# Flamingo block on one core: queries of two batches at once, P times V by head pairs, the mean of V from an added zero row

## The reference, cut to what matters

```python
# x (32, 224, 512), ctx (32, 750, 384), mask (32, 224): True where a query is kept
x = x + tanh(g_xattn) * attention(layernorm(x), ctx, mask)
x = x + tanh(g_ffn) * bit_ffn(layernorm(x))

# attention, 16 heads of 32
q = (x @ Wq.T), k, v = split(y @ Wkv.T)
attn = einsum('bhnd,bhmd->bhnm', q * scale, k)
attn = where(pad_mask[:, None, :, None], attn, -1e9)   # a row that isn't kept: all scores equal
out = einsum('bhnm,bhmd->bhnd', softmax(attn), v)      # ... so it gets the mean of V
```

## Time and profile before

| | |
|---|---|
| median of three runs | 2137.53 us |
| profiled execution | 2138.34 us, span of its trace 2136.5 us |
| PE busy | 1908.6 us (89%) |
| DVE, ACT, POOL busy | 1278.7 us, 1067.5 us, 557.7 us |
| first part | PE from 27.59 to 1593 us |
| second part | from 1597.09 us to the end |

### The profile page before, as it was taken

How to read it: one execution, slowest core, us unless ns; L and a number is a source line. 1 busy time by engine, 2 the same in 40 slices (tenths; PEclk the granted TensorE clock), 3 DMA queues, 4 the chain that set the end, 5 groups by cost and what they waited for, 6 DMA issues and landing times. The chain is left out here.

```text
span 2136.5 us, 47614 instructions
## 1 busy us (share of the span) xinstructions
PE 1908.6 (89%) x17554; PEld 1489.4 (70%) x17611; DVE 1278.7 (60%) x2524; ACT 1067.5 (50%) x1923; POOL 557.7 (26%) x621
## 2 busy tenths in 40 slices
PE   4999999989999997999899979999966888888887
PEld 4888888868888886778778867888753444444443
DVE  4445454434445544545454544555448999999996
ACT  3344444434434443334344433444326888888887
POOL 2101011010101111111111111112006777777774
PEclk9999999989999998999999989999978999999999
DMA  3021111131211113111111031111212222222221
GB/s 107 29 70 37 38 37 38 37 90 38 69 41 37 37 37 89 37 38 37 38 58 51 26 90 47 37 38 37 65 34 90 85 88 88 88 88 86 81 84 55
DMA packets 56158, 122.65 MB, mean 57 GB/s; under 512 B 5527, under 2 KB 5527, under 8 KB 55864
## 3 DMA queue, kind: packets, MB, share of 16 engines
q1 hardware_dynamic: 55992, 120.07, 17.5%
HBM read 101.63 MB, written 29.43 MB: 61 GB/s over the span
## 5 line engine op out<-in xcount | busy, mean ns | idle before, releaser
L565 DVE TENSOR_TENSOR k_l<-psum,k_h 128x376 fp32r<-128x376 f32 (+1 forms) x256 | 140.1, 547 | 339.6 <-ACT k_h L395 339.2
L560 DVE TENSOR_REDUCE nmax<-psum 112x1 f32<-112x750 f32 x256 | 228.4, 934 | 189.7 <-PE psum L757 189.7
L404 ACT ACTIVATE prob<-psum,nmax 112x750 f32<-112x750 f32 x256 | 224.8, 882 | 232.0 <-DVE nmax L560 232.0
L337 POOL TENSOR_SCALAR x_var<-x_mv 56x1 f32<-56x1 f32 x32 | 8.1, 253 | 1218.1 <-DVE x_mv L538 1218.1
L395 ACT ACTIVATE k_h<-psum 128x376 fp32r<-128x376 f32 (+1 forms) x256 | 123.8, 484 | 339.6 <-PE psum L768 339.6
L768 PE MATMUL psum<-y_h,wkv_h 128*128 128x376 f32 (+1 forms) x768 | 277.3, 361 | 0.0
L778 PE MATMUL psum<-wkv_h,y_h 128*125 128x512 f32 x576 | 250.8, 435 | 27.4 <-DVE q_l L553 27.4
L768 PE MATMUL psum<-y_l,wkv_h 128*128 128x376 f32 (+1 forms) x768 | 255.8, 333 | 0.0
L768 PE MATMUL psum<-y_h,wkv_l 128*128 128x376 f32 (+1 forms) x768 | 255.7, 333 | 0.0
L1280 PE MATMUL psum<-w_q,hq_t 128*128 128x512 bf16 x841 | 192.9, 382 | 62.0 <-DVE hq_t L1183 62.0
L778 PE MATMUL psum<-wkv_l,y_h 128*125 128x512 f32 x576 | 236.7, 411 | 0.0
(11 more groups left out here) (123 smaller groups left out, 3485.1 us busy)
## 6 DMA issues: line engine op xcount, KB each, us to landing
y<-in_ctx_t SPq DMA_DIRECT2D x32, 1125.0 KB, 6.2
w_part<-in_w_t SPq DMA_DIRECT2D x32, 512.0 KB, 4.9
xb<-in_x SPq DMA_DIRECT2D x56, 256.0 KB, 2.7
ab<-attn_rows SPq DMA_DIRECT2D x56, 256.0 KB, 2.9
out_rows<-yo SPq DMA_DIRECT2D x56, 256.0 KB, 2.1
attn_rows<-vmean_rows SPq DMA_DIRECT2D x32, 336.0 KB
xa<-in_x SPq DMA_DIRECT2D x32, 112.0 KB
attn_rows<-attn SPq DMA_DIRECT2D x32, 112.0 KB
```

The costliest lines, as they stand in the source:

```text
L404: act.activation(prob[:, e, :], ps_score[e][0:RP], ACT.Exp, bias=nmax[:, i:i + 1], accum_out=den[:, i:i + 1]).then_inc(p.exp, 1)
L560: dve.tensor_reduce(nmax[:, i:i + 1], ps_score[e][0:RP], AX.X, ALU.max, negate=True).then_inc(p.max, 1)
L565: dve.tensor_tensor(k_l[:, g, s0:s1], ps_proj[k_bank[g, hf]][:, 0:s1 - s0], k_h[:, g, s0:s1].bitcast(F32), ALU.subtract).then_inc(a_kl, 1)
```

## The change

- The 56 rows of `x` of two batches are loaded, normalised, transposed and multiplied by Wq together, once for a pair of batches. Each batch gets one more row between, which is zero: `RM = R + 1 = 57` rows, `RP = 114` for a pair. For DVE the normalisation falls in even periods, the query matmuls and the split of q in odd ones.
- A zero row of `x` gives equal scores, so row 57 of each batch's output is the mean of V. `y_sum`, the group's matmuls and `after_group` go. In each period SP stores the 56 rows and the mean row, waits until both have landed, and issues the DMA that spreads the mean over 168 rows.
- P times V works on pairs of heads: 12 matmuls a group instead of 24, with 64 columns of V as weights and 114 columns moving. Half of each result is not wanted (head 0 of V with head 1 of P); `heads_out` on DVE picks the diagonal with two instructions (L618, L620) where one copy stood.
- The first scores of a period wait for the first two K pieces only, `k0 - (2 * NG - 2)`; what follows waits for the others.
- The programs of even and odd periods are written apart. K piece (1, 1) comes ahead of the V pieces 3 and 4 on PE, `k_half(1, 1)` and `v_chunk(3)` ahead of `normalise` on DVE, and two of ACT's three `next_y` ahead of the third softmax pair.
- The nested loops become two single ones with a `middle` between them, in which the mean of the absolute weights is made.

```diff
-    RP = 2 * R
+    RM = R + 1
+    RP = 2 * RM
...
+                def results(b):
+                    sp.wait_ge(last.on, b + 1 + ONE)
+                    sp.dma_start(rows(attn_d, b, RB), attn[0:R, :]).then_inc(last.st, 16)
+                    sp.dma_start(vmean_d[bass.ds(b, 1), :], attn[R:RM, :]).then_inc(last.st, 16)
+                    sp.wait_ge(last.st, 32 * (b + 1) + ONE)
                     sp.sem_inc(met_sp, 1)
-                    with sp.Fori(0, QTR) as t:
-                        b = sp.snap(q * QTR + t)
-                        f = sp.value_load(kind[0:1, bass.ds(b, 1)])
-                        with sp.If(f > 1):
-                            sp.sem_inc(a_fill, 16)
-                        with sp.Else():
-                            sp.dma_start(rows(attn_d, b, 0, RB), vmean_d[bass.ds(b, 1), :].to_broadcast([RB * R, D])).then_inc(a_fill, 16)
-
-                sp.wait_ge(a_flag, 4)
-                batches(sp, period, fills)
+                    sp.dma_start(rows(attn_d, b, 0, RB), vmean_d[bass.ds(b, 1), :].to_broadcast([RB * R, D])).then_inc(a_fill, 16)
...
+                def heads(p, n):
+                    act.wait_ge(p.q, n + 1 + ONE)
+                    for s in range(2):
+                        for e in range(2):
+                            act.activation(q_h[:, s, :, e, :], ps_q[:, :, RM * s:RM * s + RM], ACT.Copy,
+                                           scale=head_col[:, e:e + 1]).then_inc(p.qh, 1)
...
-                    dve.tensor_copy(o_t[:, g, :], ps_o[:, g, :]).then_inc(p.oe, 1)
-
-                def divided(p, n):
+                    dve.tensor_scalar(o_t[:, g, :], ps_o[:, g, 0:RM], head_one[:, 0:1], 1.0, ALU.mult, ALU.mult).then_inc(own_o, 1)
+                    dve.wait_ge(own_o, 1)
+                    dve.scalar_tensor_tensor(out=o_t[:, g, :], in0=ps_o[:, g, RM:RP], scalar=head_one[:, 1:2], in1=o_t[:, g, :],
+                                             op0=ALU.mult, op1=ALU.add).then_inc(p.oe, 1)
+                    dve.sem_clear(own_o)
...
+                def even(b, t, late):
...
+                    heads_out(last, b, 1)
+                    if more_pairs(t, 1):
+                        moments(last, t + 1, 32 * (t + 2) + ONE)
+                    weights(b, late)
+                    k_half(m, 0, 1, 1)
+                    v_chunk(m, 0, 1, 3)
+                    if more_pairs(t, 1):
+                        normalise(last, t + 1, (t + 1) * (2 * NBLK) + RB)
+                    second_half(last, n1, 2, 0)
+                    second_half(last, n1, 2, 1)
+                    negated_max(last, n0, 3, 0)
+                    negated_max(last, n0, 3, 1)
+                    heads_out(last, b, 2)
...
                     for j in range(MJ):
-                        for h in range(HPG):
-                            w = 128 * g + HD * h
-                            mm = pe.matmul(ps_o[HD * h:HD * h + HD, g, :], v[:, slot, j, w:w + HD],
-                                           prob_t[:, g % 2, h // 2, j, R * (h % 2):R * (h % 2) + R],
+                        for e in range(2):
+                            w = 128 * g + PW * e
+                            mm = pe.matmul(ps_o[PW * e:PW * e + PW, g, :], v[:, slot, j, w:w + PW], prob_t[:, g % 2, e, j, :],
                                            start=(j == 0), stop=(j == MJ - 1))
...
-                def ordered(b, j, q, attends, projects):
-                    n0 = b * NP + ONE
-                    m = b + 1
-                    here, ahead = j, (j + 1) % 2
-                    pe.wait_ge(a_kl, 2 * NG * m + ONE)
-                    if attends:
+                def even(b):
+                    n0, m = b * NP + ONE, b + 1
+                    k0 = 2 * NG * m + ONE
+                    pe.wait_ge(last.ql, 2 * b + 4 + ONE)
+                    pe.wait_ge(a_kl, k0 - (2 * NG - 2))
+                    pe.wait_ge(last.pa, n0)
+                    pe.wait_ge(last.pd, n0)
+                    scores(last, 0, 0)
+                    pe.wait_ge(a_yl, CC * (b + 2) + ONE)
+                    pe.wait_ge(a_kl, k0 - 1)
+                    v_chunk(0, 1, 0)
+                    pe.wait_ge(a_kl, k0)
+                    k_half(0, 1, 0, 0)
...
+                    scores(last, 0, 2)
+                    weighted(last, n0, 0, 1)
+                    pe.wait_ge(a_va, MH * m + 2 + ONE)
+                    k_half(0, 1, 1, 1)
+                    pe.wait_ge(a_kl, k0 + 3)
+                    v_chunk(0, 1, 3)
+                    turn_prob(last, n0, 2, 0)
+                    turn_prob(last, n0, 2, 1)
+                    pe.wait_ge(a_kl, k0 + 4)
+                    v_chunk(0, 1, 4)
+                    turn_out(last, b, 1)
+                    pe.wait_ge(last.pa, n0 + 6)
+                    pe.wait_ge(last.pd, n0 + 6)
+                    scores(last, 0, 3)
```

More of the change, by code:

```diff
@@ L344, in _, with period @@
                 rstd(last, 0)
-                def period(b, j, q, t):
+                def period(b, j, t, late):
+                    if j == 0 and more_pairs(t, 1):
+                        rstd(last, t + 1)
                     if loads_ahead(b):
-                        rstd(last, b + 2)
                         split_y(b + 2, j)
-                batches(pool, period, lambda q: None)
+                batches(pool, period, lambda: None)
                 def slow(b, n):
@@ L459, in ordered @@
                     if projects:
-                        k_half(m, 2, 0)
-                        k_half(m, 2, 1)
+                        k_half(m, 1, 2, 0)
+                        heads(last, t + 1)
                     if attends:
@@ L498, in slow @@
                         turned(rest, i)
-                        heads(rest, i, 0)
+                        heads(rest, i)
                         for g in range(NG):
@@ L621, in ordered, with odd @@
+                def odd(b, t, late, attends, projects):
+                    n0, n1, m = b * NP + ONE, b * (2 * NP) + ONE, b + 1
                     if attends:
@@ L645, in ordered @@
                         heads_out(last, b, 1)
-                    if ahead:
-                        moments(last, b + 2)
-                    if has_part(b):
-                        weights(b, q, t, j)
-                    if ahead:
-                        normalise(last, b + 2, (b + 2) * NBLK + RB)
+                        weights(b, late)
                     if projects:
-                        heads(last, m, slot)
-                        k_half(m, 1, 1)
+                        k_half(m, 1, 1, 1)
+                        v_chunk(m, 1, 0, 3)
                     if attends:
@@ L692, in after_group, with period, middle @@
+                        k_half(m, 1, 3, 0)
+                    if attends:
+                        divided(last, b, 32 * b + ONE)
+                    if projects:
+                        k_half(m, 1, 3, 1)
+                def period(b, j, t, late):
+                    if j == 0:
+                        even(b, t, late)
+                    else:
+                        odd(b, t, late, has_part(b), projects_ahead(b))
+                def middle():
                     dve.tensor_reduce(w_sum[:], w_sums[:, 0:4 * DC].rearrange("p (i c) -> p i c", i=2), AX.X, ALU.add).then_inc(a_wsum, 1)
-                    dve.wait_ge(a_wmm, q + 1 + ONE)
+                    dve.wait_ge(a_wmm, 1 + ONE)
```

649 lines of the change are left out of this document (360 added, 289 removed).

## The result

The changed kernel took 2026.88 us (median, 2025.12 to 2028.69), the kernel before 2137.07 in the same comparison: a ratio of 0.948 (95% interval 0.947 to 0.950). I had said 2129, with a range from 2098 to 2162. The direction was right and the size was not: the forecast missed 102 of the 110 us. Three single executions far outside (3752.9 and 3259.8 us of the kernel before, 8838.0 us of one experiment) are in none of the ratios.

A forecast was written before the change was run, and what follows sets the result against it. It took PE's stream plus PE's gaps to bound the first part. Early pairs +13, late pairs +14, last pair -1, group ends -43, ends +8 gave -9 us, so 2129 us, range 2098 to 2162.

The forecast's parts named there:

- The gap before even periods: PE's first scores of even periods: 2.50 us idle at the loop's jump, and 1.5 us of slow clock, would remain.
- The new stall on DVE: PE in even periods would wait for DVE, held up by POOL's `y_l`: 1.9 us an early pair, 5.2 a late one.
- P times V: Head pairs with 114 columns take 1.33 us a group, +0.61 a group, +4.9 us a pair.
- the rival that the tiles don't overlap: The two 64-column tiles of P times V run one after the other: 2.5 us a group, total 2279; chance 0.04.
- Query: Query matmuls for two batches on PE: a pair pays 3.60 us once, -3.6 us a pair.
- First scores: The 1.15 us gap before odd periods goes, the jump before even ones remains: -1.15 us a pair, bounds 0 and -2.
- Group ends: Pairs ending a group of 8 batches lose their excess from SP's issues and the late y load: -43 us, bounds -38 and -47.
- Ends: Prologue +2, last batch +1.5, second part starting 4.5 us later: +8 us, bounds 3 and 12.
- Last pair: The last pair of periods, without POOL work: -1 us.
- DVE is never late: Rival: DVE and POOL miss each other, K (1, 1) is in time, every pair is PE-bound: 2079 to 2100; chance 0.13.
- the late wait for `k_l` before V 4: In late even periods PE waits 3.4 us before V 4 for DVE's quantised K (1, 1).
- the wait before scores 3: In even periods PE waits for DVE's `prob_t` copies before scores 3: 1.9 us early, 0.5 late.

The follow-up runs named there:

- 1809: Changed kernel, P times V as 24 matmuls of 32 weight columns: 2066.25 us with 114 moving columns, 1998.31 us with 57 and one copy per group.
- 1713: Changed kernel with P times V by single heads in three of four groups, head pairs in the fourth: 2017.95 us.
- 1665: Changed kernel with single heads in three groups of even periods and two of odd ones, `normalise` moved behind the copies: 1995.73 us.
- 1626: Kernel before with P times V over 4 of the 6 context pieces only: 2096.95 us.
- 1617: Changed kernel with P times V by single heads in two of four groups: 1992.66 us; with `normalise` moved behind the copies too, 1974.70 us.
- the shift by 128: Changed kernel, single heads in five of eight groups, `normalise` later, plus 64 small matmuls (128 instructions) ahead of TensorE's first loop: 1988.24 us against 1995.73.
- the pair of runs with equal code: Changed kernel with 24 matmuls of 32 weight columns: all 114 moving columns, 2066.25 us, against 57 moving and one copy per group, 1998.31 us.
- the best kernel here: Changed kernel with single heads in two of four groups and `normalise` moved behind the copies: 1974.70 us, 0.9231 of the kernel before.

## Why the prediction was wrong

*The gap before even periods: the step that failed.* I wrote "in even periods the jump remains" and took 2.50 us and 1.5 us of slow clock for a price of jumping. It is the price of fetching the loop's code again. The body went from 1882 to 1425 instructions, and the fetch went with it. The lengths in between (1809, 1713, 1665, 1626, 1617), the count of packets and the shift by 128 show it. In my sum it stayed in each pair with 4.0 us, taken over from the 92.5 and 95.4 of the kernel before: 15 x 4 = 60 of the 102 us. With the length alone put back the changed kernel lost 39 us, 3.6 in an early pair and 1.9 in a late one; the other 21 are gaps of about 2.0 us instead of 2.5 there and, by estimate 10 of them, the slow clock, which is absent behind most late gaps there and present in the kernel before. The row that could have told was on the page of the kernel before: 149 packets, 2.44 MB, for a first part with 13 jumps back. I never asked what they carried.

The Trainium skill bears on this, and I had not looked there. Its page "Runtime: NRT & Kernel Launch", section "Instruction fetch mechanics", says that TensorE's instruction memory takes 2048 instructions, that it is filled in blocks of 16 KiB, and that a taken branch whose target isn't in the window forces a fetch. The runs agree on the block (16 KB a packet) and on the branch (nine packets and 1.8 to 2.4 us in the changed kernel). They don't agree, for TensorE, with the same section's "only 2 cache lines" (which it works out from 32 KiB) and window of two pages, or with "Advanced Engine Details and Errata", section "ISA Cache", which says "Only 2 cache lines!" beside 128KB for TensorE: by two blocks each of these loops would be fetched again at every pass, and bodies of 1617 and 1425 instructions cost no packet. By 2048 instructions 1809 and 1713 should have stayed, and they did not, though with their 31 semaphore instructions they are only 1840 and 1744.

*The new stall on DVE: mis-sized.* I had 1.9 us a pair early and 5.2 late (with its clock); it was 0.35 and 1.68 and cost no clock: 8 x 1.55 + 7 x 3.5 = 37 us of the miss. The place was right (the scores of group 3, for DVE's copies of `prob_t`), and so was the cause: `xa` takes 1.98 us beside POOL's `y_l` instead of 0.55, and with `normalise` moved the wait is gone. That `y_l` is what makes `xa` long is read from the rows side by side (1.98 to 2.00 us beside it, 0.55 without); no run took `y_l` away. What was wrong is when POOL starts. Its `y_l` stand behind `x_var` and `x_rstd`, and these wait for DVE's moments and then take 0.71 and 1.50 us beside DVE's quantising; so the first `y_l` began at 977.73, when the third quantising step ran. None of the three waited (0.76, 0.70, 0.69 against my 0.7, 2.7, 2.1), V 4 waited for nothing, and `x_keep` took 0.19 early and 0.70 late, not 1.72. I had let three instructions meet POOL that the earlier trace rows show meeting it in another order of work.

*P times V.* 1.33 us a group, as taken; the rival that the tiles don't overlap fell. The columns cost 68 us in the pair of runs with equal code, 78 in my sum. The page on TensorE that I weighed there (the Trainium skill, "TensorE: Matmul & The Clock Gate", section LDWEIGHTS) gives 1.28 us for either form, so that this edit would cost nothing; the trace has 0.72 against 1.33 us.

*Query.* 32 rows from 666.83 to 670.39, 3.56 us (3.60 predicted), once a pair.

*First scores.* -1.15 a pair was right for odd periods. In even ones K's wait had lain under the jump; without the new wait it would have come out at 1.34 us when the jump's gap went.

*Group ends.* -43 predicted, -40 measured, and the spreading alone gave 34 in the kernel before. *Ends.* +8 predicted, +3.5 measured; the gap to the second part grew by 4.8 us as worked out (4.5), the prologue didn't grow. *Last pair.* -1 predicted, -6.7 measured; no run shows why.

*Rivals.* "DVE is never late" (2079 to 2100) came nearest and had 0.13. With the jump's 60 us dropped as well it would have said 2079 - 60 = 2019. Its mechanism was right in part only: the quantising was short, but `xa` wasn't. No case had the jump's gap vanish, so the range could not reach there: its bound for the first scores ended at -2 us a pair, and the truth was -5.2 with the clock. Of my own signs of being wrong, the 2.5 us before even periods and the late wait for `k_l` before V 4 were absent, and the wait before scores 3 was there.

*Slips in the sum.* The late terms on DVE add up to T+8.9, not T+9.2, and a query row of 0.124 us would save 3.2 us a pair, not 2.9. Neither changes the forecast by more than 2 us.

Not settled: the exact room for a body. At 1665 the place of the loop decides, 1617 stayed in both loops, 1626 in all passes but one, 1713 in none; whether each of those would do so at every place was not tried. Nor is it known why nine packets are fetched. That the clock falls behind such a gap is seen in the kernel before and in early passes, but not in most late ones of the run with 24 matmuls of 114 columns, and I haven't told apart what decides it.

## What to carry to other kernels

A gap called "issue" at a loop's head, and a queue of instructions that carries many more packets than the program is long, meant here that the loop's code was fetched again in each pass: count the body's instructions, and try the shorter form even where it streams more columns. Then weigh columns against code group by group; the best kernel here had just so many of the dear short form as it took for the body to stay. And an instruction that meets another engine's traffic costs only where a waited-for one stands behind it, so move it there first and shorten it later.

## What the hardware showed unexpectedly

- In the changed kernel a jump back over a body of 1713 or 1809 instructions fetched nine packets of 16 KB and cost 1.8 to 2.4 us of TensorE's time; with 1617 it cost neither. At 1665 one of two loops paid, and a shift of 128 instructions moved the cost to the other.
- Behind such gaps of about 2 us the granted clock fell in early passes (0.83 over 10 us) and stayed full in most late ones (1.00).
- One group's P times V (fp32, so each matmul is two rows): 48 loads of 32 columns with 56 moving take 0.72 us, 48 loads of 32 with 114 moving 1.31, and 24 loads of 64 with 114 moving 1.33. Moving columns set the time here, not the number or the width of the loads.
- DVE's `x_keep`, one element a row, took 0.14 to 0.20 us, 0.70, 1.63 or 1.72; each of the long ones ended as a `y_l` of POOL did.
